# A three-layer block on one core: sum of squares in three passes, and reordered work around the recurrent layer

## The reference

```python
x = x + 0.5 * ffn(layernorm(x), w_up, w_down)
x = x + rnn(layernorm(x), Wf, Wi, Wh)
x = x + 0.5 * ffn(layernorm(x), w_up, w_down)

def ternary_linear(x, w):            # w becomes -1, 0 or 1 by 0.5 * mean(|w|)
    rms = sqrt(sum(x * x, -1)) / sqrt(d)
    return einsum('bsd,fd->bsf', x / (rms + 1e-8), w_t)
ffn: h = gelu(ternary_linear(x, w_up));  ternary_linear(h, w_down)     # 128 -> 512 -> 128
rnn: f, i = sigmoid(x Wf), sigmoid(x Wi);  c = g(x Wh)
     hidden[t] = f[t] * hidden[t-1] + i[t] * c[t],  hidden[-1] = 0.5
```

## Time and profile before

| | |
|---|---|
| median of 3 runs | 303.44 us (302.75 to 303.98) |
| the profiled execution: its time, its span | 303.66 us, 301.8 us |
| TensorE busy, share | 246.6 us, 82% |
| VectorE | 254.3 us, 84% |
| ScalarE | 223.7 us, 74% |
| GpSimd | 219.5 us, 73% |
| chain that ended last | VectorE 32%, TensorE 26%, GpSimd 19%, issue 14%, ScalarE 6% |
| mean granted clock of TensorE | 0.989 |

### The profile page before, as it was taken

One profiled execution on the slowest core, in us unless ns is written; L12 is line 12 of the kernel. 1 busy time (PEld: TensorE's weight loads), 2 busy tenths in 40 slices (PEclk: granted clock), 3 DMA queues, 4 the chain that ended last, 5 costly groups with the idle time before them and its releaser, 6 DMA issues.

```text
span 301.8 us, 9838 instructions
## 1 busy us (share of the span) xinstructions
PE 246.6 (82%) x3757; PEld 168.2 (56%) x3757; DVE 254.3 (84%) x798; ACT 223.7 (74%) x546; POOL 219.5 (73%) x390
## 2 busy tenths in 40 slices
PE   0559998899989998878778775749989899999974
PEld 0337676667766776344434432327667667767753
DVE  3768999999999998787789936679999988887883
ACT  1266998798879998677776763457988789989971
POOL 5889697797887766676766777894978879776231
PEclk9999999999999999999999999798999999999999
DMA  5970000000000000000000000000111211111122
GB/s 169 297 187 3 2 3 2 3 2 4 2 3 1 4 3 2 0 2 0 2 0 0 1 0 3 1 0 2 38 37 37 72 38 39 55 55 38 37 73 72
DMA packets 18047, 9.74 MB, mean 32 GB/s; under 512 B 592, under 2 KB 17872, under 8 KB 18000
## 3 DMA queue, kind: packets, MB, share of 16 engines
q1 hardware_dynamic: 16896, 8.39, 10.3%
q10 hardware_dynamic: 1104, 0.72, 0.8%
HBM read 4.92 MB, written 4.19 MB: 30 GB/s over the span
## 4 chain that ended last, share of the span: by engine, by line
DVE 32%; PE 26%; POOL 19%; issue 14%; ACT 6%; DMA 1%; POOLq 0%; DVEq 0%; ACTq 0%
DVE h_lo L570 10%; POOL root L194 8%; DVE X L590 7%; PE U L460 6%; DVE st L549 4%; PE U L405 4%; PE T L387 3%; PE U L406 3%; PE Y L460 3%; POOL xn L215 3%; DVE xt_lo L566 3%; PE G L432 3%; DVE h_half L578 2%; POOL inject L233 2%; ACT U L296 2%
## 5 line engine op out<-in xcount | busy, mean ns | idle before, releaser
L296 ACT ACTIVATE U<-U 128x1024 f32<-128x1024 f32 x64 | 65.7, 1026 | 29.9 <-PE U L406 29.9
L570 DVE SCALAR_TENSOR_TENSOR h_lo<-U,h_hi 128x1024 f16<-128x1024 f32 x64 | 77.9, 1217 | 1.6 <-ACT h_hi L302 1.6
L215 POOL TENSOR_SCALAR xn<-X,neg_mean,rstd 128x128 f32<-128x128 f32 x164 | 72.6, 455 | 4.0 <-DVE rstd L562 1.3
L405 PE MATMUL U<-xt_hi,up_w 128*128 128x512 f16 x128 | 50.9, 398 | 19.5 <-DVE h_lo L570 16.4
L302 ACT ACTIVATE h_hi<-U 128x1024 f16<-128x1024 f32 x64 | 65.9, 1030 | 1.0
L222 POOL TENSOR_TENSOR rms<-ssq,half 128x4 f32<-128x4 f32 x32 | 34.5, 1078 | 40.6 <-ACT square_junk L328 40.6
L445 PE MATMUL Y<-down_w,h_hi 128*128 128x128 f16 x512 | 60.9, 220 | 0.0
L445 PE MATMUL Y<-down_w,h_lo 128*128 128x128 f16 x512 | 60.6, 219 | 0.0
L406 PE MATMUL U<-xt_lo,up_w 128*128 128x512 f16 x128 | 50.5, 394 | 0.0
L445 PEld LDWEIGHTS Y<-down_w,h_lo 128*128 128x128 f16 x512 | 50.1, 98 | 0.0
L445 PEld LDWEIGHTS Y<-down_w,h_hi 128*128 128x128 f16 x512 | 49.3, 98 | 1.3
(11 more groups left out here) (71 smaller groups left out, 415.9 us busy)
## 6 DMA issues: line engine op xcount, KB each, us to landing
X<-in_L_attn_x SPq DMA_DIRECT2D x16, 256.0 KB, 5.1
out_x<-X SPq DMA_DIRECT2D x16, 256.0 KB, 2.3
up_raw<-in_L_ffn_w_up ACTq DMA_DIRECT2D x1, 256.0 KB, 3.9
down_raw<-in_L_ffn_w_down ACTq DMA_DIRECT2D x1, 256.0 KB, 4.9
gate_raw<-in_L_attn_Wh ACTq DMA_DIRECT2D x1, 64.0 KB, 4.4
gate_raw<-in_L_attn_Wi ACTq DMA_DIRECT2D x1, 64.0 KB, 4.1
gate_raw<-in_L_attn_Wf ACTq DMA_DIRECT2D x1, 64.0 KB, 4.1
```

Of the source, the lines that this page charges most:

```text
L215: m = eng.tensor_scalar(xn[:, n % 2, t, :], X[:, c, :], neg_mean[l][:, c:c + 1], rstd[l][:, c:c + 1], ALU.add, ALU.mult)
L296: eng.activation(U[part][:], U[part][:], ACT.Gelu, scale=1.0 / XN_SPLIT).then_inc(gelu_done, 1)
L405: pe.matmul(U[part][:, c, :], up_w[:, f0:f0 + P], xt_hi[:, F % 2, :], start=True, stop=False)
L570: vec.scalar_tensor_tensor(out=h_lo[:, F % 2, 2 * part:2 * part + 2, :], in0=U[part][:], scalar=H_SPLIT, in1=h_hi[:, F % 2, 2 * part:2 * p ...
```

## The change

Five things change.

- In the first FFN `gram` makes three passes, h_hi.T h_hi, h_hi.T h_lo and h_lo.T h_hi, and `h_halves` does nothing there. The diagonal is then the whole sum of squares, and `rms_step` has 1 for 2 under the root. The second FFN keeps h_half and two passes.
- In both FFNs VectorE's `finish_ffn` stands between the two h_low, behind the first, and no longer ahead of both.
- ScalarE's two tiles of a group in the recurrent layer are split into `norm_tile` calls: one after the first sigmoid and one after the second. The semaphore counts both.
- For the second FFN's layer norm var_eps and neg_mean are made on VectorE (`last_moments`) behind the statistics of a link's last group, and GpSimd's `ln_roots` begins with root. var_eps[2] has a buffer per link index.
- At the end of the recurrent layer ScalarE copies group 0 of the second FFN (xt_hi) at the start of its last step and no longer behind the table load; `low_part(groups)` stands ahead of the last statistics; and part 0 of the first `up` no longer waits for the scan of group 14.

```diff
@@ ln_roots, GpSimd
-                pool.wait_ge(mv_done[l], i + 1)
-                eng.tensor_scalar(var_eps[l][:, par, 0:w], var, s * RMS_EPS ** 2, LN_EPS * s * RMS_EPS ** 2,
-                                  ALU.mult, ALU.add).then_inc(var_set[l], 1)
...
+                if l == 0:
+                    pool.wait_ge(mv_done[l], i + 1)
+                    eng.tensor_scalar(var_eps[l][:, par, 0:w], var, s * RMS_EPS ** 2, LN_EPS * s * RMS_EPS ** 2,
+                                      ALU.mult, ALU.add).then_inc(var_set[l], 1)
...
                 pool.wait_ge(var_set[l], 3 * (i + 1))
@@ rms_step, GpSimd
-                eng.tensor_scalar(rms_den[:, par, :], rms[:, par, :], 2.0 * (2.0 / dff) ** 0.5, 2.0 * H_SPLIT * RMS_EPS,
+                eng.tensor_scalar(rms_den[:, par, :], rms[:, par, :], 2.0 * ((1.0 if F < groups else 2.0) / dff) ** 0.5, 2.0 * H_SPLIT * RMS_EPS,
@@ ScalarE
-            def norm_rest(n):
+            def norm_tile(n, t):
                 g = n - groups
                 act.wait_ge(shift_done, g + 1)
                 act.wait_ge(xt_ready, n - 1)
-                for t in range(POOL_TILES, TILES):
-                    c = g * TILES + t
-                    m = eng.activation(xn[:, n % 2, t, :], X[:, c, :], ACT.Identity, bias=shift[:, c:c + 1],
-                                       scale=rstd[1][:, c:c + 1])
-                m.then_inc(xn_act_ready, 1)
+                c = g * TILES + t
+                eng.activation(xn[:, n % 2, t, :], X[:, c, :], ACT.Identity, bias=shift[:, c:c + 1],
+                               scale=rstd[1][:, c:c + 1]).then_inc(xn_act_ready, 1)
@@ ScalarE, the loop of the recurrent layer
-                if r + 1 < groups:
-                    turned(groups + r + 1)
-                for n in range(3):
-                    gate(r, n)
+                turned(groups + r + 1)
+                gate(r, 0)
+                if by_both(groups + r + 2):
+                    norm_tile(groups + r + 2, 2)
+                gate(r, 1)
+                if by_both(groups + r + 2):
+                    norm_tile(groups + r + 2, 3)
+                gate(r, 2)
                 if r == 0:
                     sum_squares(groups - 1)
-                if by_both(groups + r + 2):
-                    norm_rest(groups + r + 2)
                 if r + 4 < groups:
                     rnn_moments(r + 4)
             act.preload_act_table(ACT.Gelu)
-            turned(2 * groups)
@@ TensorE, turn and up
-                    pe.wait_ge(xn_act_ready, n - groups - 1)
+                    pe.wait_ge(xn_act_ready, 2 * (n - groups - 1))
...
-                    pe.wait_ge(scan_done, groups - 1)
+                    if part == 1:
+                        pe.wait_ge(scan_done, groups - 1)
@@ TensorE, gram
-                pe.wait_ge(h_half_done, 2 * F + 2)
+                if F >= groups:
+                    pe.wait_ge(h_half_done, 2 * (F - groups) + 2)
...
-                        for part in (h_half, h_lo):
+                        for left, right in ((h_hi, h_hi), (h_hi, h_lo), (h_lo, h_hi)) if F < groups else ((h_hi, h_half), (h_hi, h_lo)):
                             for n in range(2):
                                 i = slice(t * P + n * HALF, t * P + (n + 1) * HALF)
-                                m = pe.matmul(G[n * HALF:(n + 1) * HALF, t, 0:HALF], h_hi[:, par, c, i], part[:, par, c, i],
+                                m = pe.matmul(G[n * HALF:(n + 1) * HALF, t, 0:HALF], left[:, par, c, i], right[:, par, c, i],
@@ VectorE
+            def last_moments(i, first, n):
+                w, s = n * TILES, XN_SPLIT ** -2
+                mean, var = mv[2][:, cols(first, w), 0], mv[2][:, cols(first, w), 1]
+                dve.wait_ge(mv_done[2], i + 1)
+                vec.tensor_scalar(var_eps[2][:, i, 0:w], var, s * RMS_EPS ** 2, LN_EPS * s * RMS_EPS ** 2,
+                                  ALU.mult, ALU.add).then_inc(var_set[2], 1)
+                vec.tensor_scalar(var_eps[2][:, i, w:2 * w], var, s, None, ALU.mult).then_inc(var_set[2], 1)
+                vec.tensor_scalar(neg_mean[2][:, cols(first, w)], mean, -1.0, None, ALU.mult).then_inc(var_set[2], 1)
+
             def h_halves(F, part):
+                if F < groups:
+                    return
@@ VectorE, the loop
                     candidate(r)
+                if r == groups - 1:
+                    low_part(groups)
                 if 0 <= s - 24 < groups:
                     stats(2, s - 24)
                     mean_var(2, s - 24)
+                    i = link_of(2, s - 24)
+                    if sum(links(2)[i][1:]) == s - 24 + 1:
+                        last_moments(i, *links(2)[i][1:])
                 if in_ffn:
                     if F + 1 not in (groups, 2 * groups):
                         low_part(F + 1)
-                    finish_ffn(k, q)
                     h_low(F, 0)
                     h_halves(F, 0)
-                if in_ffn:
+                    finish_ffn(k, q)
                     h_low(F, 1)
                     h_halves(F, 1)
...
-                if r == groups - 1:
-                    low_part(groups)
```

More of the change, by code:

```diff
@@ L68, in build_macaron @@
         rstd = [sb(f"rstd{l}", [P, tiles]) for l in range(3)]
-        var_eps = [sb(f"var_eps{l}", [P, 2, 4 * TILES]) for l in range(3)]
+        var_eps = [sb(f"var_eps{l}", [P, groups if l == 2 else 2, 4 * TILES]) for l in range(3)]
         root = [sb(f"root{l}", [P, 2, 4 * TILES]) for l in range(3)]
@@ L574, in h_halves @@
             def h_halves(F, part):
+                if F < groups:
+                    return
                 dve.wait_ge(h_hi_done, 2 * F + part + 1)
-                if F >= 2:
+                if F >= groups + 2:
                     dve.wait_ge(gram_done, F - 1)
```

10 lines of the change are left out of this document (5 added, 5 removed).

## The result

The changed kernel took 294.63 us in the median of 4 runs (294.17 to 296.68), the kernel before 303.64 beside it (4 runs, 302.75 to 303.98). The ratio is 0.9721, 95% interval 0.9671 to 0.9771: 9.0 us less, where 9.75 were predicted. 293.7 was forecast, 290.3 to 298.6 the range. The profiled execution took 294.17 us, its span is 292.4.

The account below looks back on a forecast made before the run. It saw four stretches with different limits: VectorE and TensorE nearly full in the first FFN, a circulating wait in the recurrent layer. Terms -1.4 + 0.3 - 9.75 + 1.1 = -9.75 against 303.44 gave 293.7 us, range 290.3 to 298.6.

Parts of the forecast that it names:

- The circle: Recurrent layer, candidates 1 to 8: inject, rstd, shift, tile 2, sig_i, inject takes 3.68 us per group; -7.4 us.
- The moments in full rounds: Recurrent layer, candidates 8 to 11: three small instructions moved to VectorE cost 0.4 us per round, +1.2 in three.
- the round behind them: Recurrent layer, candidate 11 to 12: one set of statistics falls away, 4.70 becomes VectorE's 3.5 + 0.4; -0.75 us.
- Roots at the end: End of the recurrent layer: four single roots on the chain, each reached 0.71 us sooner; -2.8 us (-2.0 to -3.5).
- gain nothing by themselves: Start of the second FFN: moving group 16's xt_hi, xt_lo and up part 0 earlier gains nothing; VectorE's order holds h_lo.
- Gain 13 x (6.03 - 5.88) = 1.9: First FFN: 13 groups at a period of 5.88 us instead of 6.03 save 1.9 us.
- The border's +0.3: Between first FFN and recurrent layer: the later addition delays the h_lo that gates(0) awaits; +0.3 us (0 to +1.0).
- Rival B: First FFN: the third pass costs more than its pairs show; 299.7 us in total, halfway 296.7; chance 0.12.
- Second FFN: +1.1 us together: groups 1 to 7 +0.4 with moments on VectorE, last eight groups 0, last group's additions +0.7.
- Rivals C: Recurrent layer: stops at a longer circle, 4.2 us per group, +3.6; 297.3 us in total; chance 0.15.
- D: Recurrent layer: tiles do not help, 4.70 us remains (+7.4), third pass dearer (+3.0); 304.1 us in total; chance 0.03.
- E: Recurrent layer: ScalarE blocks on shift before sig_i, 5.48 us per group, +12.6; 306.3 us in total; chance 0.04.

Follow-up runs that it names:

- circle_open: The changed kernel with GpSimd's rnn_scales moved ahead of inject, so that shift no longer waits for inject: 293.20 us, ratio 0.9666 to the kernel before.
- moments_only: The kernel before with only var_eps and neg_mean of the second FFN's layer norm moved to VectorE: 302.93 us, ratio 0.9984.
- three_add: The kernel before with three passes in the first FFN and VectorE's additions between the two h_low in both FFNs: 303.02 us, ratio 0.9994.
- tiles_only: The kernel before with only ScalarE's two tiles moved behind the first and the second sigmoid: 293.89 us, ratio 0.9684.
- tile_pair_first: The changed kernel with both ScalarE tiles behind the first sigmoid: 298.89 us, ratio 0.9873 to the kernel before.
- tiles_roots_open_add: tiles_only plus single roots' moments on VectorE, rnn_scales ahead of inject, second-FFN additions between the h_low except in the last two groups: 288.55 us, ratio 0.9515.

## Why the prediction was right, and where not

**The recurrent layer** was right by its own steps. The circle was worked out from four rows of a kernel in which it did not yet bind, and came out at 3.68 where 3.66 was measured; one tile more gives 4.05, and opening it gives 3.53. The moments in full rounds were predicted at 0.4 each and cost 0.49 (1.47 for three), the round behind them -0.75 and -0.79. The first of them is the outlier, 5.46 against 5.06 for the next two: its first L568 took 0.53 us against 0.17 for the later ones, until GpSimd's inject had ended. In circle_open, where inject ends 0.13 us after L568 has started and not 0.50, L568 takes 0.17 and this round 5.06 as well.

**Roots at the end:** "each reached 0.71 us sooner" was too small. The four intervals shrank by 1.07, 0.83, 0.84 and 0.85, 3.60 together, just above the end of the range that was given for this term (3.5). The distance that counts is from the inject ahead of the three operations to root. In the kernel before it is 2.06 us, to root's start at 184.91 of the earlier trace rows from

```profile
182.85 1.26 POOL L233 TENSOR_TENSOR inject<-sig_i,cand 128x512 f32<-128x512 f32 x1 [1.22 <-DVE cand L598]
```

and with the change 1.23 (174.01 to 175.24), which is 0.83 less. Of the 0.24 more in the first interval 0.22 lie between candidate 12 and its inject (0.96 before, 0.74 after). The prediction also held that moving xt_hi, xt_lo and up "gain nothing by themselves", since VectorE binds in both orders. That holds for the old order of VectorE's waits; once the roots come sooner, moments_only shows that the path over up and h_hi binds instead, and about 0.9 of the 3.60 go with that move.

**First FFN: the step that failed** is "Gain 13 x (6.03 - 5.88) = 1.9". The 5.88 is right for undisturbed groups (5.86). What was missing is that TensorE, once it hardly waits for another engine, stands still by itself: 1.34 us of gaps up to gram 14, and 0.49 in the border. That these are waits for its own instructions is likely and not shown. The border's +0.3 came out at +0.59 (gram 14 to candidate 1), and of that 0.49 is the gap. Rival B asked whether the third pass costs more time on the array; it does not. It costs 64 more instructions per group.

**Second FFN:** +1.95 where 1.1 was predicted, and no term was right by itself. Its grams 0 to 7 cost 1.14 where 0.4 was put down; moments_only has 1.23 there, three_add -0.32, so it is the moments on VectorE that cost. From gram 7 to gram 14 the kernel gains 0.97 where 0 was put down: the groups alternate between 5.30 and 6.23 us, mean 5.77 against the 5.80 worked out, and one short interval more than long ones falls into the stretch. The last gram and its tail cost 0.83 + 0.84, where 0.7 was put down. One y_scale with its additions delays the last gram (in three_add, at the full clock, by 0.73), and the longer wait that goes with it here costs the clock on top, which is the 0.84.

**The total** was close (-9.75 predicted, -9.0 in the medians, -9.41 between the last additions of the two traces). Much of that is luck, because the errors had both signs and the start, which I cannot tie to the change, gave 1.29: first FFN +1.64, second +0.85, moments +0.23, roots -0.80, circle -0.29, start -1.29. And tiles_only says what the sum does not: one of five parts carries all of it, where the sum had counted on the roots for 2.8 us and on the three passes for 1.4.

Rivals C, D and E are refuted by 3.66 per group. E's mechanism, ScalarE blocked in front of sig_i, is real: tile_pair_first has a wait of 0.94 each round, yet the other links overlap with it, and it ends at 4.05 and not at 5.48.

## What to carry to other kernels

When no engine is full, write down the circle of waits, link by link with the durations of the present trace, and then look for the next circle that the edit closes. The second one here was predicted to 0.02 us per group, and a single swapped pair of calls on the engine that closes it opened it again. Measure each part of a bundle alone, since the other four parts here added up to nothing although two of them save time in the traces at some place, and move small work only in the rounds where the receiving engine waits.

## What was not expected of the hardware

- TensorE stood still for 0.15 to 0.91 us in mid-stream in the kernels with 96 matmuls per gram, each time until 2.26 to 2.91 us after a 16 KB block of instructions had started to arrive, and at the same three places of the program. Splitting or repeating small matmuls may have a price in instructions that no busy time shows.
- A busy share of 14.94 out of 15.00 on TensorE held 0.19 us of slack per group (turns 3.66 apart, 3.47 in circle_open), hidden under the recorded length of a matmul.
- Behind 2.07 us of waiting TensorE came back at the lower clock (0.50 granted, mask matmuls 0.42 us), behind 1.65 us in another kernel at the full one (0.30). In four kernels with a wait of 2.06 or 2.07 the clock fell, in one with 1.97 it did not. The wait on VectorE was paid twice there.
- A small instruction on VectorE (L568, 128x4) that started beside GpSimd's inject ended 0.02 to 0.04 us behind inject's end, and so took between 0.17 and 0.95 us. Beside GpSimd's root (166.75 to 168.39 in tiles_roots_open_add) the same operation took 0.16.
- Three instructions of 128x4 on VectorE start 0.07 to 0.08 us apart (167.12, 167.19, 167.26), less than half of their recorded 0.16.
